# Row-sum matmuls issued directly behind the PV matmuls of their slot

## The reference

```python
mu = jnp.mean(hidden_states, axis=-1, keepdims=True)
var = jnp.var(hidden_states, axis=-1, keepdims=True)
x = (hidden_states - mu) * jax.lax.rsqrt(var + LN_EPS) * ln_gamma + ln_beta
Q = _split_heads(x @ Wq.T)          # K and V are the heads of ctx_4096 itself
scores = jnp.einsum('bhsd,bhtd->bhst', Q, K) * scale
scores = jnp.where(mask, scores, -jnp.inf)
probs = jax.nn.softmax(scores, axis=-1)
attn = jnp.einsum('bhst,bhtd->bhsd', probs, V)
out = attn.transpose(0, 2, 1, 3).reshape(B, S, HIDDEN) @ Wout.T
return residual + out
```

## Time and profile before

| | us |
|---|---|
| median of 3 runs | 833.66 |
| lowest and highest run | 831.94, 836.31 |
| span of the profiled execution | 834.2 |
| PE busy | 734.1 (88%) |
| DVE busy | 522.4 (63%) |
| ACT busy | 395.9 (47%) |
| POOL busy | 390.7 (47%) |

### The profile page before, as it was taken

One profiled execution on the slowest core, in us unless ns is written; L12 is line 12 of the kernel. 1 busy time (PEld: TensorE's weight loads), 2 busy tenths in 40 slices (PEclk: granted clock), 3 DMA queues, 4 the chain that ended last, 5 costly groups with the idle time before them and its releaser, 6 DMA issues.

```text
span 834.2 us, 11710 instructions
## 1 busy us (share of the span) xinstructions
PE 734.1 (88%) x3585; PEld 415.4 (50%) x3585; DVE 522.4 (63%) x786; ACT 395.9 (47%) x613; POOL 390.7 (47%) x107
## 2 busy tenths in 40 slices
PE   2699999879898898789898898988989696979998
PEld 2577888434344444344344344434434343448886
DVE  5744441586776867487777767768677767563231
ACT  3631112646664665467666565666657364710000
POOL 2000000464674949096776947558594756740000
PEclk9599999999997978699999898999899798999999
DMA  9521101445141332234252241514324101303221
GB/s 327 141 53 37 51 1 39 116 106 126 40 114 49 93 77 65 53 89 105 58 118 70 71 105 36 138 35 105 76 65 99 41 26 43 110 8 144 101 90 61
DMA packets 41442, 68.43 MB, mean 82 GB/s; under 512 B 7256, under 2 KB 23656, under 8 KB 41384
## 3 DMA queue, kind: packets, MB, share of 16 engines
q1 hardware_dynamic: 41248, 67.53, 30.0%
q0 software_dynamic: 80, 0.26, 0.2%
q10 hardware_dynamic: 64, 0.01, 0.0%
HBM read 25.44 MB, written 4.19 MB: 36 GB/s over the span
## 4 chain that ended last, share of the span: by engine, by line
PE 80%; DVE 13%; issue 4%; DMA 1%; SPq 1%; ACT 1%; DVEq 0%; ACTq 0%
PE MX L880 16%; PE SX L901 16%; PE PV L917 15%; PE MX L1049 11%; PE SM L907 6%; DVE mxh L708 5%; PE PV L851 5%; PE SM L851 5%; DVE MX L699 3%; PE MX L828 2%; PE MX L887 2%; DVE MM L713 1%; DMA PR<-in_x 1%; PE MX L822 1%; DVE stats L624 1%
## 5 line engine op out<-in xcount | busy, mean ns | idle before, releaser
L699 DVE CUSTOM_DVE_ANT_0 MX<-MX,maskadd 128x1024 f32<-128x1024 f32 x256 | 310.3, 1246 | 157.6 <-PE MX L880 153.8
L573 ACT ACTIVATE PR<-SX,cols 128x512 f32<-128x512 f32 x512 | 323.3, 683 | 172.2 <-PE SX L901 167.8
L452 POOL TENSOR_TENSOR acc<-acc,PR 128x2048 f32<-128x2048 f32 x64 | 292.2, 4566 | 32.7 <-ACT PR L573 26.3
L452 POOL TENSOR_TENSOR acc<-PR 128x2048 f32<-128x2048 f32 x16 | 73.4, 4587 | 312.8 <-PE SM L907 165.8
L901 PE MATMUL SX<-R 98*128 98x512 f32 x512 | 195.6, 452 | 7.8 <-issue 5.8
L880 PE MATMUL MX<-R 96*128 96x512 f32 x512 | 171.7, 435 | 8.6 <-DVE mx L699 8.0
L901 PEld LDWEIGHTS SX<-R 98*128 98x128 f32 x512 | 97.3, 201 | 125.7 <-ACT PR L573 98.7
L917 PE MATMUL PV<-PR,C 128*32 128x512 f32 x1024 | 149.0, 656 | 0.2 <-ACT PR L573 0.2
L880 PEld LDWEIGHTS MX<-R 96*128 96x128 f32 x512 | 94.0, 200 | 102.9 <-DVE mx L699 56.3
L887 PE MATMUL MX<-ident,MM 128*128 128x128 f32 x64 | 14.0, 358 | 50.3 <-DVE MM L713 50.3
L1049 PE MATMUL MX<-R 128*128 128x512 f32 x192 | 46.2, 400 | 5.2 <-DVE R L787 5.2
(11 more groups left out here) (80 smaller groups left out, 581.9 us busy)
## 6 DMA issues: line engine op xcount, KB each, us to landing
R<-KTh SPq DMA_DIRECT2D x128, 128.0 KB, 2.3
PR<-in_x SPq DMA_DIRECT2D x16, 512.0 KB, 4.2
C<-in_ctx SPq DMA_DIRECT2D x16, 512.0 KB, 3.5
R<-KTl SPq DMA_DIRECT2D x64, 128.0 KB, 2.3
R<-QTh SPq DMA_DIRECT2D x128, 64.0 KB, 2.0
acc<-in_L_xattn_Wq SPq DMA_DIRECT2D x8, 512.0 KB, 3.4
R<-QTl SPq DMA_DIRECT2D x64, 64.0 KB, 2.0
C<-in_L_xattn_Wout SPq DMA_DIRECT2D x8, 512.0 KB, 3.2
```

The lines of the kernel that those rows point to most:

```text
L452: nc.gpsimd.tensor_tensor(acc[:, :, :], a, PR[:, tt % RING, :, :], ALU.add).then_inc(pool_used, 1)
L573: nc.scalar.activation(PR[:, tt % RING, h, :], SX[h % 2][:, :], ACT.Exp, scale=SCALE, bias=cols[:, MSK + b * TT + tt:MSK + b * TT + tt + 1 ...
L699: nc.vector.tensor_tensor_reduce(out=MX[par][:, :], in0=MX[par][:, :], in1=maskadd[:, u % BATCH, :], scale=1.0, scalar=-BIG, op0=ALU.add, ...
```

## The change

The row-sum matmuls are taken out from between the `with_23` items and put directly behind the PV matmuls, ahead of the `with_01` items and ahead of the scores of heads 2 and 3. `last_sum` moves with them. The number of instructions of every engine stays, and only PE's order differs.

```diff
--- before.py
+++ after.py
@@ -1007,21 +1007,17 @@
                     with_01, with_23 = items[tt]
                     if tt >= 1:
                         values(n, u, tt - 1)
+                        direct_sum(n, tt - 1)
                     elif not first:
                         values(n - 1, u + RING - 1, TT - 1)
+                        direct_sum(n - 1, TT - 1)
+                    if tt == SUM_SLOT and not first:
+                        last_sum(n - 1)
                     for item in with_01:
                         mx_item(*item)
                     scores(n, u, tt, 2)
                     scores(n, u, tt, 3)
-                    for item in with_23[:1]:
-                        mx_item(*item)
-                    if tt >= 1:
-                        direct_sum(n, tt - 1)
-                    elif not first:
-                        direct_sum(n - 1, TT - 1)
-                    if tt == SUM_SLOT and not first:
-                        last_sum(n - 1)
-                    for item in with_23[1:]:
+                    for item in with_23:
                         mx_item(*item)
 
             last_kinds = [item[0] for item in ORDER[-2:]]
```

## The result

| | before | after |
|---|---|---|
| median, us | 832.8 (4 runs) | 854.06 (4 runs) |
| lowest to highest | 829.84 to 836.31 | 852.74 to 859.58 |
| span of the profiled execution | 834.2 | 851.1 |

The ratio is 1.026 with a 95% interval of 1.0208 to 1.0311: the change made the kernel 21 us slower. The forecast was 863 us, with a range of 849 to 876.

What follows compares the result with a forecast made beforehand. POOL's third and fourth additions, released by ACT's exponentials, were taken to hold DVE's bias columns and so PE's bias matmuls. On 834.2 us, 26.55 for the order plus 3 for the clock gave 863.7 profiled, forecast 863 us, range 849 to 876.

Steps and rivals of the forecast that it cites:

- Slot 4, +0.99: Row sum ahead of the scores of heads 2 and 3 makes POOL's third addition 0.99 us later each step.
- Slot 1, +0.65: With `last_sum` moved, item 6 waits 0.65 us for DVE, and no PE gap absorbs it before slot 4.
- Slot 0, +0.10: Later scores of heads 2 and 3 make PE wait for exponentials: bounds 0 and 0.3 us, taken as 0.1.
- 35.6 to 35.8: Sign expected in the profile after: the length in us of a full-clock step, 33.94 before.
- steps 13 to 15: Last steps: 1.75 us more in step 13, 2.35 in step 14 without keys item, 1.7 in step 15 without max items.
- Step 0: PE already waits for DVE inside slot 4, so the row sum falls into holes: -0.3 us, bounds -0.5 and +1.0.
- The clock, +3: The longer gap before the bias matmuls makes one of three full-clock steps in ten fall more: +3 us.
- Rival A: The clock falls at each gap before the bias matmuls: 868 to 878 us, centre 871; chance 0.18.
- B: Only part of the delay reaches the chain; 0.65 or 0.99 falls out, 13 to 15 times: 849 to 854 us; chance 0.10.
- C: `L713` loses to POOL's fifth addition in all twelve loop steps: 53 us more, about 914 us; chance 0.03.
- D: Bias columns slip in before POOL's fourth addition, the gap shrinks to nearly nothing: some 805 us; chance 0.04.
- E: No change, within 0.5% of 833.7 us, item waits and score delays falling into holes; chance 0.03.

Runs made afterwards that it cites:

- The gate: Both orders, with POOL's fourth addition of a step also waiting until DVE's bias columns are done: old order 770.33 us, changed order 783.73 us.
- slot 4 alone: Old order with 20 extra transposes in PE's gap, only the row sum of slot 4 moved behind the PV matmuls: 820.26 us, against 807.42 without the move.
- the filled one: Each order with 20 extra transposes, output overwritten, in PE's gap before the bias matmuls: old order 807.42 us, changed order 826.77 us.
- written-out pair: Both orders with PE's three loop rounds written out, other engines as before: old order 825.29 us, changed order 854.03 us.
- the three moves: Old order with 20 extra transposes in PE's gap, one row-sum move each: slot 4 820.26 us, slot 1 815.68, slot 0 808.17; none 807.42.

## Why the prediction was right, point by point

The direction, the mechanism and the range were right; the median lies 9 us below the forecast, and errors of opposite sign lie behind that number, as the sum shows.

**What bounds the kernel** held at every link: ACT releases the third addition, the third and fourth set the columns, the columns the bias matmuls. The gate showed the last link, slot 4 alone the first.

**Slot 4, +0.99,** measured 0.86. The term was mis-sized: I took the distance from the row-sum group to the next group of another shape. Behind the PV matmuls it starts 0.88 us after them, 0.12 sooner than a group of another shape.

**Slot 1, +0.65,** measured 0.51: the wait was 0.60, and the same 0.12 went off it.

**Slot 0, +0.10,** measured 0.02. A full-clock step therefore became 1.36 us longer and not 1.75: the filled one takes 35.32, below the 35.6 to 35.8 that I had named as a sign. In steps 13 to 15 I expected 1.75, 2.35 and 1.7 us, together 5.8; in the two profiles they grew by 6.26.

**The sum** was 29.55 us with the clock, and the profiled execution grew by 16.9. Of the 12.6 us between them, steps 1 to 12 without step 5 make 4.95 (forecast 11 x 1.75 + 3 = 22.25, measured 17.30), step 5 makes 9.44 (+1.75 against -7.69), and the other parts go the other way by 1.8. Step 0 is one of them: I had -0.3, and it took 0.98 us more (in the written-out pair 1.0 less, so its sign stays open). With the loop written out the pair is 28.7 us apart, close to 29.55, but not because the terms were: the order costs 19.4 us in the filled pair where I added up 26.55, and the rest is some 9 us, where I had 3 for the clock.

**The clock, +3.** The same ten steps take 340.59 and 353.34 us in the filled kernels. Above that lie 357.21 - 340.59 = 16.6 us before and 372.43 - 353.34 = 19.1 after, so +2.5 between these two profiles; with the loop written out it is 8.6 us over twelve steps, so +3 was too low there. Rival A had the right mechanism, since after the change all ten steps lie at 0.91 to 0.95, and too high a price: each of the ten costs 1.9 us on average, not 2.55. Its range, 868 to 878, was missed.

**What I did not see** is the 5.83 us stall in the profiled execution of before, in the step of 45.52 us that I left out of the ten. It belongs to the time that I added the sum to, and the changed kernel did not have it: with the low clock around it that step became 7.7 us shorter. The forecast silently assumed that it would stay. With the loop written out in both, the 21 us between the medians became 28.7.

**Rivals.** B (a term falls out) is refuted by the steps of the three moves, although its 849 to 854 lie closer to the measured 854.06 than my 863: by the number alone it would have looked right; C did not come, L713 passes in 0.17 us in the loop and was late in steps 13 and 14 as before; D did not come, since the change moved DVE only 0.37 us closer to the hole (1.70 to 1.33 late). Its price, 28 us below before, looks too low: where the gate lets the columns through first, the changed order lies 51 us below before (783.73 to 835.22) and the old one 65, steps 13 and 14 included, which lost their second wait too. The gate also holds POOL, so it is not D itself. E is refuted by the 2.6%.

## What to carry to other kernels

When an instruction takes many times its shortest duration, ask who else ran until the moment it ended; its wait may be another engine's work, and holding that back by a semaphore can be worth more than the order of the bound engine, here 65 us against 21. Work that separates two uses of a double buffer is a cover: moved elsewhere, it can cost its cover even though no instruction is added, unless a gap behind it absorbs the wait. And before adding a sum to a profiled time, look for single events in it that the other program need not repeat.

## What the runs showed that I had not expected

Two groups of 32-column matmuls into different PSUM tiles start 0.88 us apart, a group of another shape 0.97 to 1.00 behind such a group.

PE can stand 5.8 to 7.5 us at a loop's branch, in some rounds and not in others, with nine more packets on the instruction queue for each stall (17, 26, 35). With 20 extra transposes in a step the steps behind the branch took 34.9 instead of 34.0 with the old order, and no long stall was seen in those profiles (18 packets in each of the filled kernels). Why some rounds stall was not settled.
